# The end of a transformer layer with a routed feed-forward: four blocks of items at the end instead of three, and a last block that is normalised and stored in halves

## The reference, cut to what matters

```python
# attention part: B=4, T=2048, D=256, 16 heads of 16, STRIDE=8
xn  = ln(x, ln1_g, ln1_b)
q, k, v = heads(xn @ w_in.T + b_in)
scores  = where(row % 8 == 0, q @ k.T / 4, only the diagonal)   # other rows attend to themselves alone
x1  = x + softmax(scores) @ v @ w_out.T + b_out
x2  = x1 + gelu(ln(x1, ln2_g, ln2_b) @ w1.T + b1) @ w2.T + b2    # "M", MLP 256 -> 1024 -> 256
y   = layernorm(x + x2)
# routed part: 8 experts, rank 4
e   = argmax(y @ gate_W.T + gate_b)
out = relu(y @ wi_W.T + wi_b + (y @ lora_A[e].T) @ lora_B[e].T) @ wo_W.T + wo_b     # "F"
result = layernorm(y + out)
```

## Time and profile before

| | |
|---|---|
| time, median of 3 runs | 1577.69 us (1573.98 to 1577.94) |
| time of the profiled execution | 1577.34 us |
| its span, first to last instruction | 1575.5 us |
| TensorE matmuls busy | 1467.2 us, 93% of the span |
| VectorE, ScalarE, GpSimd busy | 831.5, 729.3, 653.6 us |
| share of the chain that ended last | TensorE 72%, VectorE 10%, GpSimd 4%, ScalarE 4% |
| mean granted TensorE clock | 0.971 of full |

### The profile page before, as it was taken

One profiled execution on the slowest core, in us unless ns is written; L12 is line 12 of the kernel. 1 busy time (PEld: TensorE's weight loads), 2 busy tenths in 40 slices (PEclk: granted clock), 3 DMA queues, 4 the chain that ended last, 5 costly groups with the idle time before them and its releaser, 6 DMA issues.

```text
span 1575.5 us, 26420 instructions
## 1 busy us (share of the span) xinstructions
PE 1467.2 (93%) x10166; PEld 1082.4 (69%) x10166; DVE 831.5 (53%) x1786; ACT 729.3 (46%) x1071; POOL 653.6 (41%) x536
## 2 busy tenths in 40 slices
PE   4799999999999999999999999999999999999866
PEld 3587755568878666568878765567888865566765
DVE  6655466636555465545655566454746555552320
ACT  3244455553434554454444555454444455455322
POOL 1463321328745313146764422233864431313444
PEclk9999999999999999999999999999999999999978
DMA  7565122205651223103672131311672213210100
GB/s 182 167 190 121 35 60 59 64 19 186 194 122 47 51 52 71 32 32 118 205 165 72 34 73 26 70 41 49 199 205 67 75 37 60 50 24 14 54 14 14
DMA packets 102973, 132.08 MB, mean 84 GB/s; under 512 B 18888, under 2 KB 79248, under 8 KB 99728
## 3 DMA queue, kind: packets, MB, share of 16 engines
q1 hardware_dynamic: 102848, 130.39, 30.7%
HBM read 68.87 MB, written 61.36 MB: 83 GB/s over the span
## 4 chain that ended last, share of the span: by engine, by line
PE 72%; DVE 10%; POOL 4%; ACT 4%; SPq 3%; issue 3%; DMA 3%; POOLq 0%; DVEq 0%; ACTq 0%
PE ps L1366 18%; PE ps L1368 14%; PE ps L1367 14%; PE ps L1542 6%; PE ps L1531 6%; PE ps L1516 5%; DVE mx L1279 3%; PE ps L1587 2%; PE ps L1578 2%; PE ps L1606 2%; ACT gel L1065 2%; SPq L743 1%; PE ps L1548 1%; DMA k_d<-kst 1%; POOL rows L918 1%
## 5 line engine op out<-in xcount | busy, mean ns | idle before, releaser
L1279 DVE TENSOR_REDUCE mx<-ps 128x2 f32<-128x1024 f32 x256 | 313.2, 1223 | 246.6 <-PE ps L1516 245.6
L1029 ACT ACTIVATE prob<-ps 128x1024 f32<-128x1024 f32 x256 | 262.3, 1025 | 219.9 <-PE ps L1531 219.8
L927 POOL TENSOR_TENSOR hid0l<-gel,hid0h 128x512 fp32r<-128x512 f32 x86 | 112.2, 1305 | 222.8 <-ACT hid0h L1071 222.8
L927 POOL TENSOR_TENSOR hid2l<-gel,hid2h 128x512 fp32r<-128x512 f32 x85 | 110.7, 1303 | 215.1 <-ACT hid2h L1071 215.1
L927 POOL TENSOR_TENSOR hid1l<-gel,hid1h 128x512 fp32r<-128x512 f32 x85 | 110.7, 1302 | 214.3 <-ACT hid1h L1071 214.3
L1063 ACT ACTIVATE gel<-ps,cols 128x512 f32<-128x512 f32 x128 | 88.2, 689 | 199.2 <-PE ps L1368 190.8
L1542 PE MATMUL ps<-prob,vals 128*32 128x256 f32 x2048 | 165.7, 396 | 2.2 <-ACT prob L1029 2.2
L1531 PEld LDWEIGHTS ps<-qslot,kslot 50*128 50x128 f32 x1024 | 77.2, 187 | 82.0 <-issue 55.9
L1531 PE MATMUL ps<-qslot,kslot 50*128 50x256 f32 x1024 | 130.3, 333 | 3.3 <-ACT prob L1029 3.3
L1065 ACT ACTIVATE gel<-ps 128x512 f32<-128x512 f32 x128 | 76.4, 597 | 115.3 <-PE ps L1606 113.5
L1516 PE MATMUL ps<-kslot,qslot 48*128 48x512 f32 x512 | 113.1, 438 | 13.3 <-DVE mx L1279 10.7
(11 more groups left out here) (230 smaller groups left out, 3978.6 us busy)
## 6 DMA issues: line engine op xcount, KB each, us to landing
k_d<-kst SPq DMA_DIRECT2D x192, 128.0 KB
kslot<-k_d SPq DMA_DIRECT2D x64, 384.0 KB
xin<-in_L_attn_x SPq DMA_DIRECT2D x32, 256.0 KB, 4.0
x1in<-x_d SPq DMA_DIRECT2D x16, 512.0 KB, 6.4
rows<-xs_d SPq DMA_DIRECT2D x16, 512.0 KB, 5.4
out<-rows SPq DMA_DIRECT2D x16, 512.0 KB, 4.9
y_d<-rows SPq DMA_DIRECT2D x15, 512.0 KB, 3.1
rows<-y_d SPq DMA_DIRECT2D x15, 512.0 KB, 4.3
```

The source lines that it names most:

```text
L927: nc.gpsimd.tensor_tensor(hid[i % RING][1][:], gel[i % 2][:], hid[i % RING][0][:], ALU.subtract).then_inc(lo_done, 1)
L1029: nc.scalar.activation(prob[(n - 1) % 2][:].rearrange("p e i q -> p (e i q)"), ps[:, 0:2, :].rearrange("p a n -> p (a n)"), ACT.Exp).then_ ...
L1279: nc.vector.tensor_reduce(best[:, :, j % NQ], ps[:, MX:MX + 2, :], AX.X, ALU.max).then_inc(maxr_done, 1)
```

## The change

1. The block ("F", 3, 2) leaves the last attention stage and is computed in the tail, between ("M", 3, 0) and ("F", 3, 0). The last attention stage then has two blocks like the first one, the tail has four: `first`, `middle`, `third`, `last`. The three steps before a block (turning, gate, choice) are written beside the items of the block in front.
2. In the last batch entry the out-projection's sum is written straight into the attending rows' half of `x1in`; only the other half is loaded from HBM, and the store of `x1g` and the wait for it are gone. The steps `l2a`, `l2b` and `tn` of `middle` are written beside the items 4 to 7 of `first`.
3. `la` and `lb` of `middle` are written beside items 2 and 4 of `third`, the turning and gate of `last` beside items 5 to 7 of `third`; nothing is drained in between.
4. The last block is summed, normalised and stored in two halves: steps `fa` (VectorE: sum, statistics; GpSimd: the power) and `fb` (VectorE: normalisation; SyncE: store).

The core of the diff (the lines that allocate semaphores and unpack names are left out):

```diff
-    _beside = [("F", _b, 1)] + ([("F", _b - 1, 0)] if _b else []) + [("F", _b, 2)]
+    _beside = [("F", _b, 1)] + ([("F", _b - 1, 0)] if _b else []) + ([("F", _b, 2)] if _b + 1 < B else [])
...
-BLOCKS += [("F", B - 1, 3), ("M", B - 1, 0), ("F", B - 1, 0)]
-PHASE += [("tail", B - 1)] * 3
+BLOCKS += [("F", B - 1, 3), ("M", B - 1, 0), ("F", B - 1, 2), ("F", B - 1, 0)]
+PHASE += [("tail", B - 1)] * 4
...
-        items(first, {0: chain[0], 1: chain[1], 2: chain[2], 3: chain[3], 4: [("l2l", middle)], 5: [("ld", middle)], 7: [("l2a", middle)]}, first - 1)
-        put(("l2b", middle))
-        put(("tn", middle, 0))
-        put(("tn", middle, 1))
-        items(middle, {}, first)
-        drain()
-        put(("la", middle))
-        put(("lb", middle))
-        put(("tn", last, 0))
-        put(("tn", last, 1))
-        put(("xw", last))
-        put(("ga", last))
-        put(("pick", last, 0))
-        put(("pick", last, 1))
-        put(("pi", last))
-        items(last, {}, -1)
-        drain()
-        put(("la", last))
-        put(("lb", last))
-        put(("st", last))
+        items(first, {0: [("l2l", middle)] + chain[0], 1: chain[1], 2: chain[2], 3: chain[3], 4: [("l2a", middle)],
+                      5: [("ld", middle), ("l2b", middle)], 6: [("tn", middle, 0)], 7: [("tn", middle, 1)]}, first - 1)
+        items(middle, {0: [("ld", third)], 3: [("tn", third, 0)], 4: [("tn", third, 1), ("xw", third)], 5: [("ga", third)],
+                       6: [("pick", third, 0), ("pick", third, 1)], 7: [("pi", third)]}, first)
+        items(third, {2: [("la", middle)], 4: [("lb", middle)], 5: [("tn", last, 0)], 6: [("tn", last, 1), ("xw", last), ("ga", last)],
+                      7: [("pick", last, 0), ("pick", last, 1), ("pi", last)]}, -1)
+        items(last, {}, third)
+        while pending:
+            i = pending.pop(0)
+            put(("dn", i, 0))
+            put(("dn", i, 1))
+        for h in range(2):
+            put(("fa", h))
+        for h in range(2):
+            put(("fb", h))
...
-                    sp.dma_start(tiles_of(x1in[:]), x1_d[bb, :, :, 2 * n:2 * n + 2, :]).then_inc(x1ld, 16)
+                    if n == 0 and bb == LAST:
+
+                        sp.dma_start(tiles_of(x1in[:])[:, :, 1, :], x1_d[bb, :, :, 1, :]).then_inc(x1ld, 16)
...
-                    nc.vector.tensor_tensor(flat(x1g[:]), flat(x1g[:]), ps[:, BANK[(what, *a)], :], ALU.add).then_inc(x1g_done, 1)
+                    x1 = tiles_of(x1in[:])[:, :, 0, :] if b == LAST else x1g[:]
+                    nc.vector.tensor_tensor(x1, x1g[:], ps[:, BANK[(what, *a)], :].rearrange("p (t d) -> p t d", t=NQ), ALU.add
+                                            ).then_inc(x1g_done, 1)
...
+                elif what == "fa":
+                    h = a[0]
+                    k = len(BLOCKS) - 1
+                    y = rows[ROW_OF[k]][:, 2 * h:2 * h + 2, :]
+                    dve.wait_ge(half_done if h == 0 else down_done, FT * (k + 1))
+                    if h == 0:
+                        dve.wait_ge(xw_done, N("xw", k))
+                    nc.vector.tensor_tensor(flat(y), flat(y), ps[:, DOWN + h, :], ALU.add).then_inc(fsum_done, 1)
+                    dve.wait_ge(fsum_done, h + 1)
+                    for t in range(AT):
+                        nc.vector.bn_stats(astats[:, h, t, :], y[:, t, :]).then_inc(fstat_done, 1)
+                    dve.wait_ge(fstat_done, AT * (h + 1))
+                    for t in range(AT):
+                        nc.vector.bn_aggr(amv[:, h, t, :], astats[:, h, t, :]).then_inc(faggr_done, 1)
+                    dve.wait_ge(faggr_done, AT * (h + 1))
+                    nc.vector.tensor_scalar(avare[:, h, :], amv[:, h, :, 1], EPS, None, ALU.add).then_inc(fvare_done, 1)
+                elif what == "fb":
+                    h = a[0]
+                    y = rows[ROW_OF[len(BLOCKS) - 1]]
+                    dve.wait_ge(frstd_done, h + 1)
+                    for t in range(AT):
+                        at = AT * h + t
+                        nc.vector.tensor_scalar(y[:, at, :], y[:, at, :], amv[:, h, t, 0:1], arstd[:, h, t:t + 1],
+                                                ALU.subtract, ALU.mult).then_inc(fnorm_done, 1)
```

37 lines of the change are left out of this document (29 added, 8 removed).

## The result

| | before | changed |
|---|---|---|
| time, median | 1577.69 us (3 runs) | 1550.81 us (3 runs, 1548.89 to 1553.47) |
| profiled execution: time, span | 1577.34, 1575.5 us | 1553.47, 1551.7 us |
| mean granted TensorE clock | 0.971 | 0.980 |
| first to last exponential of b = 3 | 189.7 us | 153.6 us |
| start of the last exponential to start of TensorE's last matmul | 112.0 us | 127.8 us |

The ratio of the mean times is 0.9838, with a 95% interval from 0.9806 to 0.9871: the changed kernel is 1.3 to 1.9% faster. The forecast was 1546, the range 1541 to 1556, and "faster by over 0.3%" had a chance of 0.95. The median lies in the range, 4.8 us above the forecast; the profiled execution, against which the sum was made, lies 7.4 us above it. The last three rows of the table are the three terms of the prediction's sum. Measured they are -36.1, +15.8 and -4.8 (predicted: -33.9, +7.0, -4.3).

A forecast was written before the change was run, and what follows sets the result against it. TensorE's work was taken to bound the kernel, plus a hole in the long attention stage and two in the tail. Stage -33.9, later end of TensorE +7.0, end -4.3 sum to -31.2: 1546.1 us, range 1541 to 1556.

The forecast's parts named there:

- The block that leaves the stage: Last attention stage, b = 3: without the block it takes b = 0's 155.8 us instead of 189.7, saving 33.9.
- the hole: Stage of b = 3: TensorE waits 2.38 us for a row maximum behind `pick`, then 10 us at half clock; 7.4 us.
- Middle's start: Tail: the power waits for GpSimd's normalisation, TensorE waits 2.7 us or more; item 0 of `middle` ends at 1489.5.
- I take 0.5: Start of `middle`: VectorE's four normalisations beside GpSimd's subtractions lose 0.5 us; 2.6 by the skill's rule.
- The rest of `middle`: Tail: seven items, turning, gate and `pi` of `third`, and 0.5 of waiting for GpSimd; 23.5 us, to 1513.0.
- `third`: Tail: eight items 24.4, plus 3.3, 1.5 waiting at the gate and 0.6 for `pick`; 29.8 us, to 1542.8.
- half clock in the tail lasts or comes again behind the 1.5 us wait of `third`: Rival for the tail: 10 us more at half clock cost 5; 1551 to 1553, 1556 if twice; chance 0.10.
- The end: From TensorE's last matmul to the end of the span: 8.1 us instead of 12.4, 4.3 saved.
- The hole didn't return in the last stage: Rival for the last attention stage: `pick` meets a row maximum there too, adding 7.4 us, 1553.5; chance 0.07.
- The stage shrank with its items: Rival: 64 attention steps have a length of their own, so nothing is saved, 1580.0; chance 0.02.
- that rival: Rival: the whole tail stays at half clock, 75 us more, 1621; decides from 31 us of work; chance 0.03.
- The signs of being wrong: Last attention stage longer than 164 us, or clock 0.50 for more than some 10 us in the last 100 us.

The follow-up runs named there:

- run 6: Kernel before with only the block moved into the tail between `middle` and `last`, drains, x1 and end as before: ratio 0.9975, 1569.73 us.
- run 4: Changed kernel with x1's power and normalisation earlier, turns and gate of `last` apart, and `xw` later for `third` and `last`: ratio 0.9740, 1533.61 us.
- run 9: Run 4's kernel with the choice put ahead of the row maxima in the attention stages with three blocks: ratio 0.9682, 1526.74 us.
- run 3: Changed kernel with `xw` of `third` moved from item 4 to item 7 of `middle`, behind the choice: ratio 0.9806, 1544.51 us.
- its control: The changed kernel with no edit, run again beside run 10's kernel: ratio 0.9825, 1549.05 us.
- 1: Changed kernel with x1's power ahead of GpSimd's normalisation of the block in front, x1's normalisation and turns one item earlier: ratio 0.9788, 1540.59 us.
- 5: Changed kernel with the second half of `pick` put behind another step's row maxima in all four attention stages: ratio 0.9880, 1556.39 us.
- 8: Changed kernel with x1 through HBM again (store, wait, load of both halves): ratio 0.9831, 1548.73 us.
- 10: Changed kernel with the two turns of `middle` one item later, beside item 7 of `first` and behind it: ratio 0.9823, 1549.02 us.
- run 7: Kernel before with only the last block summed, normalised and stored in halves: ratio 0.9970, 1570.47 us.
- run 2: Changed kernel with turns of `last` beside items 4 and 5 of `third` and its gate beside item 6: ratio 0.9833, 1546.40 us.
- 4 again: Run 4's kernel once more, as the neighbour of run 9's on the chip: ratio 0.9733, 1535.35 us.

## Why the prediction was right, step by step

| step of the sum | predicted | measured |
|---|---|---|
| attention stage of b = 3 | -33.9 | -36.1 |
| last exponential to the end of item 0 of `middle` | 38.5 | 40.2 |
| rest of `middle`, with turns, gate and `pi` of `third` | 23.5 | 26.7 |
| `third`, with those of `last` | 29.8 | 33.4 |
| `last` and the last two `dn` | 27.3 | 27.6 |
| end | -4.3 | -4.8 |

The predicted 38.5 is 1489.5 less 1451.0; the measured ones are the differences between 1416.2, 1456.38, 1483.08, 1516.52 and 1544.14. The four middle rows miss by 1.7 + 3.2 + 3.6 + 0.3 = 8.8 us, and the stage and the end gain 2.7 back, which leaves 6.1. The other 1.3 us of the 7.4 by which the profiled time misses lie in front: the first exponential of the stage was later by so much in this execution (1262.6 against 1261.3). So the time fell in the range although the tail grew by more than twice the forecast, because the range had room above for a hole and for half clock, and the half clock is what came.

*The block that leaves the stage*: right, and shown by run 6, which has nothing else. Two readings behind its size were off. The stage of b = 0, taken as the model, wasn't clean: its mean clock of 0.99 hid some 3.5 us at half, the end of a stretch that began before the stage did (at 186.1) and ended at 189.6. The window of the kernel before:

```profile
184.00:190.00 6.00, 6.00 (x22) 4.47 (x22) 0.66 (x4) 3.50 (x4) 0.00 (x0) 0.52 0.02 5
```

In the changed kernel that window has clock 1.00, and the stage of b = 0 takes 154.2 instead of 155.8. This isn't the change's doing: in run 4, whose program is the same up to there, the window is at half again and the stage takes 155.8. It explains 1.6 of the 2.2 us, and the four transposes, named as the upper bound, 0.5. And a block of items costs a stage 184.0 - 154.2 = 29.8 us with full clock (the stages of b = 1 and b = 0 in run 9), not 27.7, so the hole was 36.1 - 29.8 = 6.3 and not 7.4. That the two errors nearly cancelled is luck as far as the adding up goes; the term itself didn't hang on it, because it was taken from whole stages. What the other 2.1 us of a block are wasn't looked into.

*Middle's start*: the mechanism was right. TensorE came to the turn 25.7 us behind the last exponential (1441.59 and 0.28, less 1416.2; predicted 25.5), the power began at 25.6 (predicted 25.6), and the half clock cost 2.2 us, between the bounds of 0 and 3.4. The step that failed is the price of the contention: "I take 0.5" was 2.1, which is 3.50 for the four normalisations less the 1.38 that they took before. The Trainium skill (SBUF — State Buffer, Who interferes with whom) says of VectorE in a 2-port mode that the one that comes second is blocked for the whole instruction, and the prediction worked out 2.6 us by it and set it aside, because the trace of before was taken to have no group of four that was held twice. The trace of the changed kernel agrees with the page in the blocking; that the normalisations are in a 2-port mode, no run here shows. And the reason given for the low price, "twice in a group of four it does not", was false for the kernel before too. I had read it off the maximum of 1436 ns, which is that of one instruction. The group at the start of the program, in VectorE's and GpSimd's timelines of the kernel before, stood in the very order that the change makes, and was held twice:

```profile
111.44 3.36 DVE L1182 TENSOR_SCALAR x1in<-x1in,mv,rstd 128x256 f32<-128x256 f32 x4 [1.13 <-POOL rstd L912]
```

```profile
111.37 1.31 POOL L927 TENSOR_TENSOR hid1l<-gel,hid1h 128x512 fp32r<-128x512 f32 x1
113.33 1.31 POOL L927 TENSOR_TENSOR hid2l<-gel,hid2h 128x512 fp32r<-128x512 f32 x1 [0.65 <-ACT hid2h L1071]
```

That is 3.36 us against the 3.50 measured later; it was there to be read.

*The rest of `middle`*: the wait of 0.5 for GpSimd came (0.60). The step that failed is that only this would be lost. `pick` has two items here, 5.6 us, for the 3.64 that it took before, but its two comparisons were held for 4.6 and 0.9 us. TensorE waited 2.56 us, and some 3 us at half clock followed. Without `xw` among them they are held for 1.0 and 1.1 and the wait is gone: run 3 shows the cause by taking it away, and run 6 by having it (4.80 and 2.54 us). The prediction named `xw` as work on GpSimd, and didn't ask whom it would hold.

*`third`*: "1.5 of waiting" was exact, and the cover of `middle`'s sum and normalisation held (no wait for them). The 0.6 in front of `pi` didn't come; TensorE was at half clock by then, so the item in front took longer. The rival "half clock in the tail lasts or comes again behind the 1.5 us wait of `third`", with a chance of 0.10, is what happened, in the small: 7 us at half, 3.5 lost, and 1.1 behind the wait for `pi`. What was said against it, over 15 us of unbroken work on either side, was no reason: in all seven profiles with this order (the changed kernel, its control and runs 1, 3, 5, 8 and 10) 3 to 7 us at half clock followed this wait.

*The end*: right; 7.56 us instead of 8.1, alone as in the whole (run 7). The last normalisation ended 5.0 us behind TensorE (predicted 4.7), and the store of the second half, issued at 1549.12, took 2.6 us to the end of the span where 3.4 had been put down: the half of the bytes was quicker by 0.8.

*The other rivals.* The hole didn't return in the last stage (window at clock 1.00). The stage shrank with its items. The tail had 14.5 us at half clock, half of the point from which that rival decides (31). The direct way for x1, counted as "isn't what they are used for", was worth nothing (run 8).

*The signs of being wrong.* The stage took 153.6 us, at full clock, well under the 164 named. The sign for the tail was clock 0.50 "for more than some 10 us" in the last 100 us. With work going on it was 3.0 + 7.0 = 10 us there, and 14.5 in the whole tail, so by this sign the prediction of the tail stood at the edge. Two things that it named didn't hold: there was a wait of over 2 us behind the start of `middle` (2.56), and the last matmul came at 1544.0 and not near 1536.

The sum of the parts alone, 0.25% and 0.30% (runs 6 and 7), is a third of the whole change's 1.6 to 1.75%. The rest comes with what runs 6 and 7 leave out: the start of `middle` written beside the items of `first`, and its sum and normalisation with the turns, gate and choice of `last` beside those of `third`. The tail of 142.6 us in run 6 is 127.8 in the changed kernel. This part wasn't run alone.

## What to carry to other kernels

When a step moves beside other work, look at what GpSimd has queued there: price a small VectorE operation by the whole row of GpSimd instructions that can stand back to back over it, and look up groups in the old trace that were in that place, not the maximum of one instruction. And take the model of a stage from a stretch whose clock you have looked at in short windows: a mean of 0.99 over 157 us hid some 3.5 us at half. Where an edit of order by itself can't be told from nothing in the time, as in run 2, look whether its wait is gone from the timeline, and try it together with others: together such edits took back the 15.8 us by which the tail had grown, and one more, in stages that the change never touched, gave 8.6.

## What the runs showed of the hardware

- A VectorE comparison of 128x32 numbers with both inputs in SBUF, 0.19 us by itself, was held 4.82 us, through three GpSimd instructions that followed each other without a gap (2.41, 1.30 and 1.30 us). A reduction (1479.62, 0.19 us) ran unhindered inside a subtraction that held the comparison behind it, and so did four statistics of x1 (1430.43, 1.41 us, their usual time) beside this addition:

```profile
1430.55 1.30 POOL L918 TENSOR_TENSOR xg<-xg,x1in 128x512 f32<-128x512 f32 x1
```

  The Trainium skill (SBUF — State Buffer, Who interferes with whom) states that a VectorE instruction with two SBUF inputs contends with GpSimd's reads and a reduction doesn't; the trace agrees, and shows that the block doesn't end with one GpSimd instruction.
- GpSimd's own normalisations didn't hold VectorE. In run 1 the four on VectorE (2.46 us) were held by the subtraction at 1431.30 and not by what GpSimd started at 1432.59, while they still ran:

```profile
1432.59 3.83 POOL L928 TENSOR_SCALAR rows<-rows,mv,rstd 128x256 f32<-128x256 f32 x3
```

  By this a VectorE step beside these costs less than beside an addition or a subtraction of GpSimd.
- Half clock came behind a wait of only 1.50 us (7 us long), with full work on both sides, and in seven profiles out of seven. It didn't come behind one of 1.58 or 1.59 in front of `pi` of `last`, in four out of four (runs 2, 4, 4 again and 9). In run 2 it didn't come behind one of 2.55 either, behind which 3 us followed in the changed kernel. Behind one and the same wait of 2.7 us it lasted about 10 us in one execution and 3.6 in another. What decides it is open.
